# A group-normalised 1x1 convolution with per-sample mixed weights: another opening, with one chunk normalised on GpSimd

## The reference

```
pooled = mean(g, axis=(2, 3))
h = relu((pooled @ fc_w.T - abn_m) * abn_g / sqrt(abn_v + eps) + abn_b)     # 32 values
ch_att, fl_att = sigmoid(h @ ch_w.T + ch_b), sigmoid(h @ fl_w.T + fl_b)     # 512 and 512
kn_att = softmax(h @ kn_w.T + kn_b)                                         # 4
agg_w = einsum('bk,koc->boc', kn_att, weight)                               # 512 x 512
y = einsum('bchw,boc->bohw', g * ch_att, agg_w) * fl_att
out = x + (y - bn_m) * bn_g / sqrt(bn_v + eps) + bn_b
```

## Time and profile before

| | us |
|---|---|
| median of 3 runs | 2090.37 |
| lowest, highest | 2088.69, 2090.68 |
| profiled execution | 2088.51 |
| its span (first to last instruction) | 2086.7 |
| PE busy in it | 2051.4 |
| DVE busy | 1896.0 |
| ACT busy | 1725.0 |

### The profile page before, as it was taken

How to read it: one execution, slowest core, us unless ns; L and a number is a source line. 1 busy time by engine, 2 the same in 40 slices (tenths; PEclk the granted TensorE clock), 3 DMA queues, 4 the chain that set the end, 5 groups by cost and what they waited for, 6 DMA issues and landing times.

```text
span 2086.7 us, 33082 instructions
## 1 busy us (share of the span) xinstructions
PE 2051.4 (98%) x10848; PEld 1060.8 (51%) x10848; DVE 1896.0 (91%) x3063; ACT 1725.0 (83%) x2307; POOL 11.2 (1%) x20
## 2 busy tenths in 40 slices
PE   4999999999999999999999999999999999999999
PEld 2555555555555555555555555555555555555554
DVE  8899999999999999999999999999999999999974
ACT  5888888888888888888888888888888888888885
POOL 0100000000000000000000000000000000000000
PEclk9999999999999999999999999999999999999999
DMA  9976655656555665556565556655566655566522
GB/s 350 291 213 207 206 200 192 204 202 211 196 194 197 205 210 201 203 189 204 205 211 193 194 196 208 211 198 204 187 205 208 209 196 194 193 211 211 176 106 106
DMA packets 241612, 422.52 MB, mean 202 GB/s; under 512 B 7472, under 2 KB 240432, under 8 KB 241584
## 3 DMA queue, kind: packets, MB, share of 16 engines
q1 hardware_dynamic: 237888, 415.74, 58.2%
q0 software_dynamic: 3696, 6.42, 1.9%
HBM read 216.61 MB, written 211.94 MB: 205 GB/s over the span
## 4 chain that ended last, share of the span: by engine, by line
PE 98%; DVE 1%; DMA 1%; SPq 0%; issue 0%; ACT 0%; DVEq 0%
PE product L877 32%; PE product L875 32%; PE product L876 32%; DMA x_ring<-x 1%; PE small L842 0%; PE product L897 0%; PE product L898 0%; PE product L890 0%; SPq L216 0%; DVE mixed_weight L649 0%; DVE chunk_stats L465 0%; DVE mean_var L499 0%; DVE x_ring L789 0%; DVE head_products L563 0%; DVE logits L568 0%
## 5 line engine op out<-in xcount | busy, mean ns | idle before, releaser
L875 PE MATMUL product<-x_hi,w_hi 128*128 128x448 f16 x3552 | 1251.9, 352 | 1.3 <-issue 1.3
L877 PE MATMUL product<-x_hi,w_lo 128*128 128x448 f16 x3552 | 1251.9, 352 | 0.0
L876 PE MATMUL product<-x_lo,w_hi 128*128 128x448 f16 x3552 | 1251.9, 352 | 0.0
L307 ACT ACTIVATE y<-product,out_bias,out_scale 128x448 f32<-128x448 f32 x892 | 637.8, 716 | 249.9 <-PE product L877 244.3
L286 ACT ACTIVATE x_norm<-x_ring,norm_bias,norm_scale 128x448 f32<-128x448 f32 x892 | 668.0, 750 | 0.0
L479 DVE TENSOR_TENSOR x_ring<-x_ring,y 128x896 f32<-128x896 f32 x432 | 463.0, 1083 | 80.4 <-ACT y L307 76.1
L875 PEld LDWEIGHTS product<-x_hi,w_hi 128*128 128x128 f16 x3552 | 350.1, 99 | 325.7 <-issue 6.9
L877 PEld LDWEIGHTS product<-x_hi,w_lo 128*128 128x128 f16 x3552 | 347.5, 98 | 323.4
L876 PEld LDWEIGHTS product<-x_lo,w_hi 128*128 128x128 f16 x3552 | 347.5, 98 | 320.7 <-issue 1.7
L465 DVE BATCH_NORM_STATS2 chunk_stats<-x_ring 128x6 f32<-128x448 f32 x896 | 491.3, 610 | 9.0 <-DMA x_ring<-x 6.8
L473 DVE TENSOR_TENSOR x_lo<-x_norm,x_hi 128x1792 f16<-128x1792 f32 x222 | 447.5, 2016 | 15.5 <-ACT x_hi L295 15.4
(11 more groups left out here) (93 smaller groups left out, 327.2 us busy)
## 6 DMA issues: line engine op xcount, KB each, us to landing
x_ring<-x SPq DMA_DIRECT2D x224, 896.0 KB, 4.8
out<-x_ring SPq DMA_DIRECT2D x216, 896.0 KB, 3.8
out<-y SPq DMA_DIRECT2D x7, 896.0 KB, 9.2
out<-x POOLq DMA_DIRECT2D x7, 896.0 KB, 12.5
weight<-wt SPq DMA_DIRECT2D x8, 512.0 KB, 12.9
out<-x_ring SPq DMA_DIRECT2D x4, 224.0 KB, 1.9
params<-par SPq DMA_DIRECT2D x1, 462.0 KB, 12.1
```

The source lines that it names most:

```text
L307: nc.scalar.activation(y[:, s % 2, t], acc[k % BANKS][:, 0:COLS], ACT.Identity, bias=obias[:, t:t + 1], scale=oscale[:, u, t:t + 1]).then_ ...
L875: nc.tensor.matmul(bank, whi[:, u, t, cols], hi, start=(t == 0), stop=False)
L876: nc.tensor.matmul(bank, whi[:, u, t, cols], lo, start=False, stop=False)
L877: ins = nc.tensor.matmul(bank, wlo[:, u, t, cols], hi, start=False, stop=(t == CT - 1))
```

## The change

It rebuilds the opening and touches a few steps of the later samples.

- **Layout.** x_ring becomes [sample of the pair][tile][3136 pixels]; `ring(slot)` names the old chunk. Weights, mixed_weight, w_hi and w_lo are stored by output block, in DRAM too, so that a block of all four kernels is 8192 bytes in a row per partition.
- **Loads.** Sample one comes in 16 pieces by channel tile, one or two chunks wide (PIECES), then parameters (the group matrix is gone), four weight blocks, and sample two as before. DVE takes statistics and aggregates tile by tile.
- **Parameters.** POOL multiplies fc with the batch norm scale once (fca) and forms hbias, so that `logits` has one step instead of three before the heads; the heads' bias is a 33rd column. `norms` waits for fca_ready in the opening, and norm_bias is now last in it.
- **Order of ACT, DVE and PE in the opening.** See the diff. `top` has four calls of 2048 elements. oscale is computed late, and ACT waits for oscale_ready before its first evacuation. 
- **GpSimd** makes x_norm of the chunk s=1 in four instructions of 448 columns, behind catt_ready; ACT made it before. Its x_lo on DVE and the reload of its ring slot wait for first_xn_ready.
- **PE** runs high passes alone as soon as w_hi is there, then the w_lo passes, then x_lo. keep_awake: 40, 5, 9 instead of 22, 0, 6.
- **Turn 0.** Statistics of chunks 14 and 15 move from (6,1) and (6,2) to (3,2) and (5,0), those of 16 from (6,3) to (6,2).
- **The DVE loop** is opened by `nc.Fori(..., head_slot=0)` instead of `dve.Fori`.

```diff
+        PIECES = [(0, 0, 1), (0, 1, 3), (0, 3, 5), (0, 5, 7), (1, 0, 2), (1, 2, 4), (1, 4, 6), (1, 6, 7),
+                  (2, 0, 1), (2, 1, 3), (2, 3, 5), (2, 5, 7), (3, 0, 2), (3, 2, 4), (3, 4, 6), (3, 6, 7)]
+            for j, (t, n, end) in enumerate(PIECES):
+                cols = slice(n * COLS, end * COLS)
+                sp.dma_start(xs[:, 0, t, cols], x_d[0, :, t, cols]).then_inc(piece_in[j], 16)
+            sp.dma_start(pa[:, :], par).then_inc(params_in, 16)
+            for o in range(CT):
+                sp.dma_start(w[:, o], wt[:, o]).then_inc(weight_in[o], 16)
+            for slot in range(CHUNKS, RING):
+                load(1, slot)
...
+            guess(start, 0)
             top(0)
             top(1)
-            guess(start, 0)
-            for j in range(2, 6):
-                top(j)
-            first_hi(0, 0)
             exponentials(start, 0)
-            top(6)
-            top(7)
-            for t in range(1, CT):
-                first_hi(0, t)
+            top(2)
             mix_first(1)
-            weight_hi(0)
+            first_hi(0, 0)
+            top(3)
             mix_first(2)
-            first_hi(1, 0)
-            first_hi(1, 1)
+            first_hi(0, 1)
+            first_hi(0, 2)
+            first_hi(0, 3)
+            weight_hi(0)
             weight_hi(1)
-            first_hi(1, 2)
-            first_hi(1, 3)
+            for t in range(CT):
+                first_hi(1, t)
             mix_first(3)
             weight_hi(2)
-            norm(start, 1, 0, True)
-            norm(start, 1, 1, True)
             weight_hi(3)
-            norm(start, 1, 2, True)
-            norm(start, 1, 3, True)
             for t in range(CT):
                 norm(start, 2, t, True)
             split(start, 2)
+            act.wait_ge(oscale_ready, 1)
...
+            def piece_stats(j):
+                t, n, end = PIECES[j]
+                dve.wait_ge(piece_in[j], 16)
+                for n in range(n, end):
+                    ins = nc.vector.bn_stats(bst[:, 0, t, n], ring(n)[:, t])
...
+            dve.wait_ge(fca_ready, 1)
             norms(start, 0)
...
+            dve.wait_ge(bn_ready, 1)
+            first_norm(0)
+            logits(start, 0)
+            attentions(start, 0)
             dve.wait_ge(att_ready, 1)
-            for half in range(2):
-                dve.wait_ge(weight_in[half], 16)
-            step(nc.vector.tensor_scalar(mix[:, :, 0:P], w[:, 0, :, 0:P], katt[:, 0:1], None, ALU.mult))
+            dve.wait_ge(weight_in[0], 16)
+            step(nc.vector.tensor_scalar(mix[:, 0], w[:, 0, 0], katt[:, 0:1], None, ALU.mult))
             add_kernel(0, 1)
-            dve.wait_ge(abs_done, 2 * KERNELS)
+            add_kernel(0, 2)
+            add_kernel(0, 3)
+            add_kernel(1, 1)
+            add_kernel(1, 2)
+            dve.wait_ge(abs_done, CT)
             nc.vector.reduce_sum(wsum1[:, :], wsum[:, :], AX.X).then_inc(wsum_ready, 1)
-            add_kernel(0, 2)
+            add_kernel(1, 3)
             dve.wait_ge(top_moved, 1)
             nc.vector.reduce_max(wtop[:, :], top_row, AX.X).then_inc(wtop_ready, 1)
-            add_kernel(0, 3)
+            first_norm(1)
             dve.wait_ge(top_moved, 2)
...
+            nc.vector.tensor_scalar(catt[:, :], sig[:, 0:CT], wscale[:, 0:1], W_TOP, ALU.mult,
+                                    ALU.mult).then_inc(catt_ready, 1)
             step(nc.vector.tensor_scalar(wscale[:, :], wscale[:, :], W_TOP, None, ALU.mult))
...
+            add_kernel(2, 1)
             dve.wait_ge(catt_ready, 1)
             first_split(0)
-            add_kernel(1, 2)
-            add_kernel(1, 3)
-            add_kernel(2, 1)
+            add_kernel(2, 2)
             first_split(1)
-            add_kernel(2, 2)
             add_kernel(2, 3)
             add_kernel(3, 1)
-            first_split(2)
             add_kernel(3, 2)
             add_kernel(3, 3)
-            first_norm(0)
-            first_norm(1)
-            first_split(3)
             first_norm(2)
             first_norm(3)
+            first_split(2)
             dve.wait_ge(xn0_ready, CT)
             dve.wait_ge(first_hi_ready, CT)
             nc.vector.tensor_tensor(xlo0, xn0, xhi0, ALU.subtract).then_inc(lo_ready, 1)
+            first_split(3)
+            step(nc.vector.tensor_scalar(inv[:, :], inv[:, :], wall[:, 0:1], 1.0 / (W_TOP * X_SCALE), ALU.mult, ALU.mult))
+            after(start)
+            nc.vector.tensor_tensor(oscale[:, 0], sig[:, CT:2 * CT], inv[:, :], ALU.mult).then_inc(oscale_ready, 1)
             dve.wait_ge(first_hi_ready, 2 * CT)
-            dve.wait_ge(xn_ready, 2)
+            dve.wait_ge(first_xn_ready, 1)
             nc.vector.tensor_tensor(xlo[:, 1], xn[:, 1], xhi[:, 1], ALU.subtract).then_inc(lo_ready, 1)
...
                 whole = {(0, 0): 7, (0, 1): 8, (0, 2): 9, (0, 3): 10, (2, 2): 11, (2, 3): 12, (3, 0): 13,
-                         (6, 1): 14, (6, 2): 15, (6, 3): 16}
+                         (3, 2): 14, (5, 0): 15, (6, 2): 16}
...
+            pool.wait_ge(norm_ready, 1)
+            pool.wait_ge(abs_done, CT)
+            pool.wait_ge(catt_ready, 1)
+            for t in range(CT):
+                ins = nc.gpsimd.tensor_scalar(xn[:, 1, t], ring(1)[:, t], nscale[:, 0, t:t + 1], nbias[:, 0, t:t + 1],
+                                              ALU.mult, ALU.add)
+            ins.then_inc(first_xn_ready, 1)
...
+            def first_products():
+                for o in (0, 1):
+                    for t in range(CT):
+                        first_high(0, o, t)
+                    for t in range(CT):
+                        first_weight_low(0, o, t)
                 for t in range(CT):
+                    for o in (0, 1):
+                        first_high(1, o, t)
+                        first_weight_low(1, o, t)
+                for s in (0, 1):
+                    for t in range(CT):
+                        first_high(s, 2, t)
+                for s in (0, 1):
+                    for t in range(CT):
+                        first_weight_low(s, 2, t)
+                for t in range(CT):
+                    first_high(0, 3, t)
+                first_low(0, 0)
+                for t in range(CT):
+                    first_weight_low(0, 3, t)
+                for o in range(1, CT):
+                    first_low(0, o)
+                for o in range(CT - 1):
+                    first_low(1, o)
+                for t in range(CT):
+                    first_high(1, CT - 1, t)
+                    first_weight_low(1, CT - 1, t)
+                first_low(1, CT - 1)
```

More of the change, by code:

```diff
@@ L215, in load @@
                 n = slot % CHUNKS
[L216 to L220, removed]
-                    for j in range(2 * KERNELS):
-                        k, half = divmod(j, 2)
-                        two = slice(half * CT // 2, (half + 1) * CT // 2)
-                        sp.dma_start(w[:, k, two], wt[:, k, two]).then_inc(weight_in[j], 16)
-                load(slot // CHUNKS, slot)
+                sp.dma_start(ring(slot), x_d[b, :, :, n * COLS:(n + 1) * COLS]).then_inc(chunk_in[slot], 16)
+            for j, (t, n, end) in enumerate(PIECES):
[6 more added lines that the diff above has]
+                load(1, slot)
             def refill(s):
@@ L568, in logits @@
                 step(nc.vector.tensor_reduce(z[:, :], prod[:, :, :], AX.X, ALU.add))
-                after(turn)
-                step(nc.vector.tensor_tensor(z[:, :], z[:, :], p_("head_bias"), ALU.add))
                 after(turn)
@@ L878, in product, with first_bank @@
+                    nc.tensor.matmul(bank, whi[:, u, o, t], lo, start=False, stop=False)
+                    ins = nc.tensor.matmul(bank, wlo[:, u, o, t], hi, start=False, stop=(t == CT - 1))
                 ins.then_inc(mm_done, 1)
-            def first_part(s, o, low):
-                k = CT * s + o
-                hi, lo = (xhi0, xlo0) if s == 0 else (xhi[:, 1], xlo[:, 1])
-                bank = acc[k % BANKS][:, 0:COLS]
-                cols = slice(o * P, (o + 1) * P)
-                if low:
-                    pe.wait_ge(lo_ready, s + 1)
+            def first_bank(s, o):
+                return acc[(CT * s + o) % BANKS][:, 0:COLS]
@@ L889, in first_part, with first_low @@
+            def first_low(s, o):
+                lo = xlo0 if s == 0 else xlo[:, 1]
+                pe.wait_ge(lo_ready, s + 1)
+                for t in range(CT):
+                    ins = nc.tensor.matmul(first_bank(s, o), whi[:, 0, o, t], lo[:, t], start=False, stop=(t == CT - 1))
+                ins.then_inc(mm_done, 1)
+            def first_products():
+                for o in (0, 1):
                     for t in range(CT):
-                        ins = nc.tensor.matmul(bank, whi[:, 0, t, cols], lo[:, t], start=False, stop=(t == CT - 1))
```

247 lines of the change are left out of this document (130 added, 117 removed).

## The result

The kernel after takes 2083.07 us (median of 7 runs, 2082.72 to 2083.93), the kernel before in the same seven rounds 2088.84 (2088.51 to 2090.91): ratio 0.9969, interval 0.9959 to 0.998. Forecast were 2087.3 and, from 2085.2 on, a range that does not hold 2083.07. The change is faster by 5.8 us, and nearly twice as much as I summed. Against the 2088.51 and 2086.7 of before, 4.6 to 5.5 us are to be found.

What follows compares the result with a forecast made beforehand. PE's single line of matmuls was taken to bound the kernel. Gains of 1.8 in the opening and 1.3 at the second sample sum to 3.1, so 2090.37-3.1 = 2087.3 us, range 2085.2 to 2090.4.

Steps and rivals of the forecast that it cites:

- The rest: Strided adds and mixes, the DVE loop's head slot, three fewer small DVE steps per sample: all beside PE, nothing gained.
- The small steps per sample: Three fewer small DVE steps in each sample: beside PE, which waited for DVE nowhere else, so nothing.
- The DVE loop's head slot: Opening of the DVE loop with a head slot: beside PE, so nothing.
- L and the transpose: L, the moment sample one's last load has landed, 19.6 instead of 20.17; transpose of the statistics 1.45 later, near 21.0.
- Newton by GpSimd's product: In the opening, DVE's Newton step is released by GpSimd's product with fc (0.40), 4.13 behind the last landing.
- t0 and the first product: t0, the start of weight_hi(0), 36.15 instead of 36.21, bound by ACT's order; PE's first product 36.7 instead of 37.24.
- The first 96 matmuls: PE up to chunk two, with waits of 0.8 and 0.4: chunk two starts at 56.5 instead of 58.28, 1.8 gained.
- The clock: In the first products: lower level cost 2.9; more fillers keep the upper level, and 1.6 returns as waits.
- GpSimd's passes: GpSimd's four x_norm passes for chunk s=1: taken as 4 us in all, at no cost.
- the slower rival: DVE's two-input instructions stand still while GpSimd makes its passes: up to 3.1 slower, 2093.5; chance 0.08.
- The second sample's first product: PE's 1.3 wait for DVE at the second sample is gained whole by moving two sets of statistics ahead.

Runs made afterwards that it cites:

- norms_back_in_after: The kernel after with the norms in the old order, norm_bias ahead of fc_pooled again: 2086.67 us, 3.4 slower than the kernel after run again.
- norms_in_before: The kernel before with only the new order of the small steps, pooled first and norm_bias behind fc_sums: 2085.10 us, 3.7 faster than before.
- padded_loop: The kernel after with the old loop without head slot, behind eight one-column memsets at DVE's start: 2082.47 us.
- plain_loop: The kernel after with the DVE loop opened the old way, without the head slot: 2108.04 us.
- control: The kernel after, unchanged, run once more beside its variants: 2083.23 us.
- old_awake: The kernel after with the old idle matmuls, keep_awake 22, 0 and 6 instead of 40, 5 and 9: 2083.30 us.
- awake_in_before: The kernel before with keep_awake of 40, 5 and 9 instead of 22, 0 and 6: 2091.07 us, 2.2 slower than before.
- act_norm: The kernel after with x_norm of chunk s=1 made by ACT again instead of GpSimd: 2084.08 us.
- statistics_back: The kernel after with the statistics of chunks 14 to 16 back at (6,1), (6,2), (6,3): 2085.20 us.
- slot_232: The kernel after with the DVE loop's first instruction at slot 232 of its fetch block instead of 0: 2097.73 us.

## Why the prediction was wrong

Wrong was the step "The rest": "all beside PE, which waited for DVE nowhere else. Nothing". The first of its items did cost nothing (the adds took 463.4 us against 463.0, the mixes 218.1 both times). The other two hold changes that work on PE.

- **The small steps per sample.** Costed at nothing; measured 3.4 (norms_back_in_after) to 3.7 us (norms_in_before). It is not that there are three fewer, since norms_in_before keeps them all; it is their new order ahead of the hidden sum. I had taken "0.16 less with norm_bias behind fc_sums" into the opening, and not asked what the same 0.16 does in the 30 samples behind it, since PE's waits had no row for it. But that view counts idle time between records, and a matmul's record overlaps the next. The weight load that fc_sums held up, "L842 PEld" with 36.6 us before against 31.1, and the group's mean of 288 ns were on the page that I read.
- **The DVE loop's head slot.** Costed at nothing; it costs 0.8 at the entry (padded_loop), and it saves 24.8 (plain_loop) that the change would else have lost, because seven DVE instructions fewer stand ahead of the loop. I had named no way in which a loop's place could cost.

Put right, the sum is 3.1+3.4-1.0 = 5.5, and 2088.84-5.5 = 2083.3; measured 2083.07. The profiles of before and control, whose spans differ by the same 5.5, divide it so: 1.6 in the opening, 1.5 at the second sample, 3.4 at the hidden sums, less 1.0 at the entry. Of the 4.2 us between the forecast and the result, though, 1.5 are not the gain at all: I had subtracted it from 2090.37, the median of three runs, and that of seven is 2088.84. Even from there, with 3.1, it would have been 2085.7. The rest of the sum, by its own steps:

- **L and the transpose.** Forecast L = 19.6 and the transpose at 21.0; the last piece landed at 20.4 (19.9 in control) and the transpose came at 22.14 (21.66). The pieces are slow at the start: 348 GB/s from 3 to 9 us, against 390 before (348 to 387 in the ten profiles with pieces, 390 to 393 in the four with chunks). Later they run faster, 397 against 382 from 6 to 19 us, so the faster rate that I had counted on is there, and the start takes it back. DVE waited 0.89 and 1.32 us for pieces two and three, and from then on had no slack for its 28 statistics and four aggregations: it, not the last landing, sets the transpose.

```profile
4.91 1.15 DVE L486 BATCH_NORM_STATS2 chunk_stats<-x_ring 128x6 f32<-128x448 f32 x2 [0.89 <-DMA x_ring<-x]
7.39 2.30 DVE L486 BATCH_NORM_STATS2 chunk_stats<-x_ring 128x6 f32<-128x448 f32 x4 [1.32 <-DMA x_ring<-x]
...
18.01 3.72 DVE L486 BATCH_NORM_STATS2 chunk_stats<-x_ring 128x6 f32<-128x448 f32 x7
...
22.14 0.21 DVE L543 STREAM_TRANSPOSE turned_mean_var<-mean_var 128x32 f32<-128x32 f32 x1
```

- **Newton by GpSimd's product.** Right in what releases it: fc_scaled, which took 0.45 (forecast 0.40). It starts at 24.80, where L = 19.6 gave 23.7, since the parameters landed at 21.4 and not at 20.6. exp_logits 4.46 behind it (4.42).

```profile
24.80 0.16 DVE L517 TENSOR_TENSOR newton<-rstd_guess 128x4 f32<-128x4 f32 x1 [0.43 <-POOL fc_scaled L850]
```

- **t0 and the first product.** ACT's order binds, as said: weight_hi(0) directly behind first_hi, 7.73 behind exp_logits (8.0). With the later transpose that is 36.99, not 36.15. The first product 0.53 behind it, as forecast.

```profile
35.04 2.05 ACT L371 ACTIVATE w_hi<-x_ring,norm_bias,norm_scale 128x448 f16<-128x448 f32 x3
36.99 2.43 ACT L385 ACTIVATE w_hi<-mixed_weight,channel_att_scaled 128x128 f16<-128x128 f32 x8
```

- **The first 96 matmuls.** Chunk two at t0+20.24 (20.35). The sum is right, its parts less so: PE's waits are 0.3, 0.2 and another 0.2 at 48.49 (two starts 0.40 apart), not 0.8 and 0.4. My terms for lo_ready add to 11.7, not to the 11.9 that I wrote; it came at 11.85. Gained in all 1.05 (profiled) to 1.57 (control), for 1.8 forecast.
- **The clock.** Upper level through, as forecast. But the "2.9 us" that I gave it as a price was never to be had: with a granted clock of 0.64 over that stretch the kernel after is as fast (old_awake), and the upper one gives the kernel before nothing (awake_in_before). I had returned 1.6 of the 2.9 as waits; all of it returns.
- **GpSimd's passes.** 3.98 us for 4, no cost, right; the contention of the slower rival is real and smaller than the slack. The Trainium skill's rule ("GPSIMD Engine Reference", "Key points") holds in part: read one by one, four of DVE's two-input instructions beside the passes grew, by 0.30 us each and one to a pass (three w_lo from 0.34 to between 0.64 and 0.69, the add from 0.74 to 1.04), and three w_lo beside them stayed at 0.34 or 0.35. GpSimd's passes also give something that I had put at nothing, since they free ACT for x_hi of chunk two: 0.85 us (act_norm).
- **The second sample's first product.** 1.3 forecast; by the distance of starts 1.51 became 0.22. statistics_back loses 2.0, of which 0.5 at a place I had not looked at.

## What to carry to other kernels

Here a small step on the way to a matmul whose operand comes just in time cost PE its early weight load, once per sample, and the waits don't show it: compare the distance of starts around such a matmul, the idle time of PEld, and the group's mean, and move ahead of it only what it needs. Whoever changes the number of instructions of an engine ahead of or inside a hardware loop has also moved the loop against the blocks in which instructions are fetched; look for an "issue" wait once per turn and for more packets in the "instruction" DMA queues, and try a few paddings or slots. A lower granted clock was no loss here, in a stretch that waits for its operands anyway; so look for what the stretch waits for before paying for the clock.

## What the runs showed of the hardware

- DVE's jump back to a loop's head, where it fetches instructions anew: 2.8 us of idle DVE (36.4 us in 13 jumps of plain_loop, 37.3 in 13 of slot_232), with 77 packets in q14. With the head eight instructions further on there is none, with 12 or 13 packets. With head slot 0 DVE stands 2.73 once, at the entry, with 13 packets.
- A pair of fp32 matmuls with 128x128 weights takes 0.11 us longer between products if its operand is ready 0.06 us ahead and not 0.19.
- GpSimd: tensor_scalar on 128x448 fp32, 1.0 us each (four in 3.98). One DVE instruction with two inputs grew by 0.30 us beside each of the four.
- Loads of 224 and 448 KB with rows of 1792 and 3584 bytes ran at 348 to 387 GB/s from 3 to 9 us (ten profiles) and at 396 to 407 from 6 to 19 us. Loads of 896 KB with rows of 1792 bytes ran at 390 to 393 and at 382 (four profiles). No run tells size, number and row length apart.
